# Opening of a sliding-window attention and gated FFN layer: the order of the first units' minima, the last rotation of keys and the first masked queries

## What is computed

```python
x = x + attn(layernorm(x), qkv_w, out_w)
x = x + ffn(layernorm(x), ...)
# attn
q = q * cos + rotate_half(q) * sin
k = k * cos + rotate_half(k) * sin
mask = (same block of 64 | first 4 rows or columns | |i - j| <= 128) & (j <= i)
attn = softmax(where(mask, q @ k.T * scale, min)); out = attn @ v
# ffn
h = silu(x @ w1.T * w1_s) * (x @ w2.T * w2_s)
h = gelu(h @ h1.T * h1_s); h = gelu(h @ h2.T * h2_s); return h @ w3.T * w3_s
```

## Time and profile before

| | us |
|---|---|
| three runs | 1075.85, 1075.22, 1078.88 |
| their median | 1075.85 |
| the profiled execution, its own time | 1075.06 |
| its span, from the first to the last instruction | 1073.2 |
| TensorE busy | 1044.7 (97% of the span) |
| VectorE busy | 629.9 (59%) |
| ScalarE busy | 701.0 (65%) |
| GpSimd busy | 440.2 (41%) |

### The profile page before, as it was taken

One profiled execution on the slowest core, in us unless ns is written; L12 is line 12 of the kernel. 1 busy time (PEld: TensorE's weight loads), 2 busy tenths in 40 slices (PEclk: granted clock), 3 DMA queues, 4 the chain that ended last, 5 costly groups with the idle time before them and its releaser, 6 DMA issues.

```text
span 1073.2 us, 20654 instructions
## 1 busy us (share of the span) xinstructions
PE 1044.7 (97%) x7218; PEld 858.8 (80%) x7218; DVE 629.9 (59%) x1940; ACT 701.0 (65%) x1680; POOL 440.2 (41%) x574
## 2 busy tenths in 40 slices
PE   6888999999999999999999999999999999999998
PEld 3556878887788877888788887888878888888887
DVE  5874577545865568555675556755577544555322
ACT  3986586945967658666687567684586946975322
POOL 5642372533724418224363245442372531532333
PEclk9989999999999999999999999999999999999999
DMA  7669879445665447555483654736556456433440
GB/s 316 252 216 277 263 226 309 130 153 179 212 179 157 141 155 247 147 161 184 133 259 93 200 167 161 236 83 213 170 166 196 124 152 205 119 90 99 157 137 21
DMA packets 112792, 190.10 MB, mean 177 GB/s; under 512 B 7216, under 2 KB 66864, under 8 KB 111664
## 3 DMA queue, kind: packets, MB, share of 16 engines
q1 hardware_dynamic: 112256, 182.45, 54.4%
q10 hardware_dynamic: 432, 6.29, 1.4%
HBM read 150.97 MB, written 45.09 MB: 183 GB/s over the span
## 4 chain that ended last, share of the span: by engine, by line
PE 85%; ACT 6%; DVE 5%; issue 2%; POOL 1%; DMA 1%; SPq 0%; POOLq 0%; ACTq 0%; DVEq 0%
PE bank L817 41%; PE bank L787 11%; PE bank L580 5%; PE bank L711 5%; PE bank L647 4%; PE bank L677 4%; PE bank L844 4%; PE bank L685 3%; PE bank L611 2%; ACT Sm L1002 2%; DVE Sm L1212 2%; PE bank L738 2%; ACT L1022 1%; PE bank L722 1%; PE bank L726 1%
## 5 line engine op out<-in xcount | busy, mean ns | idle before, releaser
L1002 ACT ACTIVATE Sm<-Sm,smin 128x260 f32<-128x260 f32 (+2 forms) x512 | 241.4, 473 | 149.9 <-DVE smin L1212 149.5
L817 PE MATMUL bank<-b_hi,W 128*128 128x512 f32 x512 | 209.4, 409 | 0.0
L817 PE MATMUL bank<-a_hi,W 128*128 128x512 f32 x512 | 206.5, 403 | 0.0
L817 PE MATMUL bank<-b_lo,W 128*128 128x512 f32 x512 | 201.1, 393 | 0.0
L817 PE MATMUL bank<-a_lo,W 128*128 128x512 f32 x512 | 200.9, 392 | 0.0
L1516 POOL TENSOR_TENSOR a_lo<-a_act,a_hi 128x512 fp32r<-128x512 f32 (+1 forms) x80 | 84.8, 1071 | 75.7 <-ACT a_hi L1052 75.7
L1212 DVE CUSTOM_DVE_ANT_0 Sm<-bank,msk,gmin 128x256 f32<-128x256 f32 x256 | 108.3, 480 | 9.3 <-PE bank L647 7.0
L817 PEld LDWEIGHTS bank<-a_hi,W 128*128 128x128 f32 x512 | 96.4, 188 | 17.5 <-ACT silu L1067 0.3
L817 PEld LDWEIGHTS bank<-a_lo,W 128*128 128x128 f32 x512 | 96.4, 188 | 17.1
L817 PEld LDWEIGHTS bank<-b_lo,W 128*128 128x128 f32 x512 | 96.6, 189 | 15.3
L817 PEld LDWEIGHTS bank<-b_hi,W 128*128 128x128 f32 x512 | 96.5, 188 | 15.1
(11 more groups left out here) (136 smaller groups left out, 2134.2 us busy)
## 6 DMA issues: line engine op xcount, KB each, us to landing
W<-w_scratch SPq DMA_DIRECT2D x168, 512.0 KB, 4.1
qk_scratch<-split SPq DMA_DIRECT2D x56, 512.0 KB, 4.0
Qs<-qk_scratch SPq DMA_DIRECT2D x112, 128.0 KB, 4.5
Ks<-qk_scratch SPq DMA_DIRECT2D x14, 1024.0 KB, 8.7
w_scratch<-in_ffn_w SPq DMA_DIRECT2D x22, 512.0 KB, 6.9
x_in<-in_x SPq DMA_DIRECT2D x8, 512.0 KB, 7.5
stage_a<-in_ffn_w ACTq DMA_DIRECT2D x2, 2048.0 KB, 9.7
x<-in_x SPq DMA_DIRECT2D x8, 512.0 KB, 3.9
```

Of the source, the lines that this page charges most:

```text
L817: mm = nc.tensor.matmul(bank[n % 2][:, :], lhsT.bitcast(F32) if general else lhsT, rhs, start=(kk == 0 and part == 0), stop=(kk == NH - 1 ...
L1002: ex = nc.scalar.activation(row, row, ACT.Exp, bias=smin[:, r, c:c + 1], scale=-1.0, accum_out=rowsum[:, i % 2, col:col + 1])
```

## The change

Two orders are changed. No instruction is added or removed.

On VectorE, the fourth rotation of sequence 0 (`rotary(0, 3)`, the keys of feature half 1, three instructions) leaves the loop ahead of `beside_attention(-1)`. It now stands in step 0 of it, behind the minima of unit 0 and of unit 1, eight instructions with their eight accumulator reads.

On GpSimd, `mask_queries(0)` goes ahead of `rotary(0, 1)`, the sum of the keys of feature half 0.

```diff
@@ beside_attention on VectorE @@
                         if r < 0 and n < UNITS and n % 2 == 0:
 
                             masked_min(a, n + 1)
+                        if r < 0 and n == 0:
+
+                            rotary(0, 2 * NF - 1)
                         if n < UNITS and (i := tile_at(n, 5)) is not None:
                             inverse_sums(a, i)
@@ VectorE, ahead of the opening @@
             dve.wait_ge(rope_loaded, 16)
-            for n in range(2 * NF):
+            for n in range(2 * NF - 1):
                 rotary(0, n)
             dve.wait_ge(msk_loaded, 16)
             beside_attention(-1)
@@ GpSimd, ahead of the opening @@
             rotary(0, 0)
+            mask_queries(0)
             rotary(0, 1)
-            mask_queries(0)
             rotary(0, 2)
             mask_queries(1)
             rotary(0, 3)
```

## The result

The changed kernel takes 1077.65 us (median of 20 runs, 1076.16 to 1082.97), and the kernel before on the same chip 1075.50 us (20 runs). The ratio is 1.0024, with a 95% interval of 1.0015 to 1.0033: slower by 2.6 us (0.0024 x 1075.5; 1.6 to 3.5 by the interval), where 2.9 was forecast. The two medians lie 2.15 us apart, and the time forecast was 1078.7. The profiled execution took 1076.37 us, its span 1074.6.

The account below looks back on a forecast made before the run. TensorE's long queue was taken to bound the kernel, starting when GpSimd's queue in the opening lets it. The median 1075.85 plus 2.9 us for the late keys, masked queries at nothing, gave 1078.7 us, range 1075.6 to 1080.8.

Parts of the forecast that it names:

- The sum: VectorE in the opening: minima 0.46 us sooner, the moved rotation behind them, so the last sum of keys 2.9 us later.
- The masked queries: GpSimd, units 0 and 1: moving them ahead gains between nothing and 0.3 us; taken at nothing.
- The two collisions: Shared port of VectorE and GpSimd: the change clears both, worth 0.27 us and 0.58 us, without altering the 2.9.
- What bounds the opening: GpSimd's unbroken queue from 21.42 to 34.2 us; all behind the last sum of keys shifts by 2.9 us.
- Rival A: TensorE's clock falls near 29 us in the longer gap, making it 3.3 to 4.9 us more together; chance 0.22.
- The second fall: TensorE's clock falls once more, slowing scores and transposes, at a cost of about 1 to 1.6 us.
- Rival B: Part is given back: no low clock at 38 us returns 1.6 us, or VectorE's saved 0.50 us counts; chance 0.15.
- C: ScalarE's queue sets the opening, so all comes 0.46 us sooner: 1075.4, or 1073.8 us; chance 0.08.
- D: Later idle time in GpSimd's queue makes up for its placements, so the time stays at 1075.85 us; chance 0.05.

Follow-up runs that it names:

- e1: The changed kernel with GpSimd's order as before, so VectorE's half of the change alone: 1077.70 us, ratio 1.0018 to the kernel before.
- e3: The changed kernel with three placements of weights on GpSimd moved ahead of its last sum of keys: 1079.64 us, ratio 1.0042.
- e12: The changed kernel with 2.8 us of extra unused products in TensorE's gap before the late keys: 1082.29 us, ratio 1.0063, 5 runs.
- e2: The kernel before with only GpSimd's half of the change, the masked queries moved ahead: 1076.89 us, ratio 1.0007.
- e4: The kernel before with three placements of weights on GpSimd moved ahead of its last sum of keys: 1079.67 us, ratio 1.0037.
- e5: The changed kernel with the last rotation four minima sooner, between those of unit 0 and unit 1: 1078.14 us, ratio 1.0026.
- e6: The changed kernel with one extra unused projection, some 1.9 us, in TensorE's gap before the late keys: 1080.00 us, ratio 1.0037.
- e9: The changed kernel with four products of zeros on TensorE ahead of the first transposes: 1075.45 us, ratio 0.9995 to the kernel before.

## Why the prediction came out right

**The sum.** Its terms held. The last sum of keys was to be 2.88 us later and is 3.00, and `Vg` 2.98. The minima's start behind the value projection, 2.54 us by the sum (23.81 - 21.27), is 2.68, since they start 0.86 us behind their scores and not 0.72. The gap of VectorE was to be 1.7 us and is 1.24. The third sine product took 0.96 us in place of 0.69: it started while GpSimd's first sum of keys was running, which the masked queries ahead of it had pushed back (they took 0.98 us beside the second sine product). It also started 0.34 us later against the value projection (0.48 behind it, 0.14 before), as the projection was shorter in this profile. In e1, e3 and e12, with projections of 9.86 us and more, it took 0.69 and the gap was 1.85. The keys do not notice: their sum is at 6.51 or 6.52 us with either gap. The moved sine product took 0.69, as assumed.

**The masked queries.** Taken at nothing, and nothing by e1 and e2. The two collisions that were to be cleared did go in this profile (0.69 us for the last sine product in place of 0.96, and no masked queries of 1.15 us), but two others came in their place, the 0.96 and 0.98 us above.

**What bounds the opening.** This step was incomplete, and the number came right without it. GpSimd's queue is the last to end, but "everything behind the last sum of keys stands in GpSimd's queue" was wrong as an explanation: by e3 VectorE's statistics, behind the load of `x_in`, come out within 0.54 us of it, and in e4, where GpSimd stood waiting for the statistics for 2.72 us, `Vg` was 4.01 us late. The prediction named that path and priced it at nothing, which is right only while both are late together. One row was also misread: of the two pieces that it calls masked queries between the placements, only the one at 30.56 is; behind the last placement come the first parts of `rstd` (L1411 and L1414 from 32.11).

**Rival A.** The fall of the clock came where it was named, from 28 us, and lasted 7 us. Its price was wrong: 0.4 us were taken for the stretch up to `Vg`, and e12 against the changed kernel shows 0.00. The second fall, priced at 1 to 1.6 us, came in e5, e6 and e9, and there the stretch behind `Vg` is 61.36 to 61.47 us against 61.07 without it: 0.3 to 0.4. The trace agrees with the Trainium skill (TensorE: Matmul & The Clock Gate, What's actually happening), by which recent activity releases the clock, in the fall behind the gap (0.60 of 4 us busy) and in the warm start (a projection of 7.10 us behind 5.76 us of products). The price is a matter of what covers the stretch.

**Rival B.** The fall at 38 us did vanish in the profile, but 1.6 us did not come back: from `Vg` to the first gated product it is 61.07 against 61.36, that is 0.29. Nor does the late opening make it vanish: e1, e5, e6 and e9 have it, some 3.4 us long as before, between 37 and 45 us. The rows suggest that ScalarE covers the low clock; no run took it alone. Its exponentials of unit 4 start at 36.99 before and 38.72 after, 1.73 later, and from there ScalarE waits for nobody until past 51 us, in either profile. Waits of ScalarE from 36 to 60 us, after:

```profile
ACT xnT L967 <- PE bank L568: 3.2, 1, 3.2
ACT Sm L1002 <- DVE smin L1212: 1.1, 1, 1.1
```

**Rivals C and D.** The first of these two waits, 0.41 us before, has grown to 3.2 us: ScalarE started earlier and gained nothing, against C. D falls with the interval, which excludes no change.

**The total.** In the profiled pair it is 1.31 us more (1076.37 - 1075.06), which is 2.98 - 0.29 less the 1.26 us by which the value projection happened to start sooner, within 0.12 us. Over 20 runs each it is 2.6 us. That this comes within 0.3 us of the forecast is in part luck. The interval runs from 1.6 to 3.5 us, and the runs of one kernel are a mixture: of the changed kernel's 20, nine had a mean granted clock of 0.994, as the profiled one, and took 1076.7 us on average, and eleven had less and took 1079.3. The stronger evidence is in the stretches of the profiles, 2.98 us up to `Vg` and 0.29 back behind it.

## What to carry to other kernels

Before moving an instruction behind others on its engine, look at whether it now runs in a gap: moved out of it, it is late by the gap and by the work put ahead of it. Here the rotation started 3.62 us later against the value projection (4.37 behind it in place of 0.75) and its sum 3.00, since before the sum had also waited 0.35 us for GpSimd and the sine product had taken 0.27 longer. All that bought was minima 0.32 us sooner, whose reader then had to wait anyway. When several queues hang on one result, taking work out of the longest shows only how near the next one is. And align two profiles at an event just ahead of the change before comparing them: here 1.26 us of 2.98 would have been lost in the start. And where runs come with their mean granted clock, look whether two medians compare the same mixture of runs.

## What was not expected of the hardware

The profile's granted clock stands at 1.00 throughout the start, but the first products of the projection take twice as long as the last: weights are loaded in 0.34 us each at first and in 0.19 later. The weight loads in the kernel before:

```profile
16.59 0.34 PEld L580 LDWEIGHTS bank<-xnT,qkv_w 128*128 128x128 f32 x1 [0.52 <-issue]
17.41 0.19 PEld L580 LDWEIGHTS bank<-xnT,qkv_w 128*128 128x128 f32 x1 [0.48 <-issue]
```

The projection takes between 8.73 us (e4) and 10.13 us (e3) in the ten profiles without products ahead of it, with the same instructions. After 5.76 us of products with zeros it takes 7.10 in all three. So at the start the durations, and not the granted clock, tell which level TensorE works at, and where the change falls is different from run to run, worth 1.4 us.

Work that fills a gap can cost more elsewhere: 2.74 us of extra products, wholly inside a wait, left `Vg` where it was and made the time 0.4% longer than that of the changed kernel (1.0063 against 1.0024). In its profile the low clock is gone from the gap and stands in later stretches; that this is the reason is not shown apart.
